# A graph layer and an expert layer on one core: later weight loads, another order in an up product, another order at the end

## The reference

```
h   = item @ W_item.T + b_item                      # 10000 x 128
x1  = x + relu(adj @ h + (layernorm(x) @ W_user.T + b_user))   # adj: 10000 x 10000
n   = layernorm(x1)
cw  = top 2 of softmax(n @ gate_w + gate_b)         # 8 experts, others 0
out = x1 + sum over e of cw[:, e] * (gelu(n @ W1[e] + b1[e]) @ W2[e] + b2[e])
```

## Time and profile before

| what | value |
|---|---|
| median of 3 runs | 1599.41 us (1597.77 to 1600.7) |
| profiled execution | 1598.91 us |
| its span in the trace | 1596.9 us |
| TensorE busy | 1575.2 us, 99% of the span |
| VectorE busy | 1491.0 us, 93% |
| ScalarE busy | 1225.2 us, 77% |
| GpSimd (POOL) busy | 68.5 us, 4% |
| granted clock of TensorE, mean | 0.998 |
| read and written | 488.31 MB, 306 GB/s |

### The profile page before, as it was taken

The page is one execution under the profiler, slowest core; times in us unless marked ns, Lnnn a source line. Parts: engine busy times, 40 slices in busy tenths (PEclk is TensorE's granted clock), DMA queues, the critical chain, the costliest instruction groups (busy, mean ns, idle before and its releaser), DMA issues.

```text
span 1596.9 us, 26046 instructions
## 1 busy us (share of the span) xinstructions
PE 1575.2 (99%) x7085; PEld 1304.3 (82%) x7085; DVE 1491.0 (93%) x2148; ACT 1225.2 (77%) x1419; POOL 68.5 (4%) x63
## 2 busy tenths in 40 slices
PE   8999999999999999999999999999999999999997
PEld 6878888888888888888888888888888888888875
DVE  6989999999999999999999999999999999999987
ACT  5778778787878777878787878777777777777866
POOL 2000000000000000000000000000000000000000
PEclk9999999999999999999999999999999999999999
DMA  9999898989898989898989898989899999989952
GB/s 371 363 324 323 299 328 299 327 299 324 290 332 287 331 290 330 284 336 280 347 281 344 282 340 292 327 296 324 298 319 310 314 315 303 323 298 326 299 201 76
DMA packets 168373, 488.31 MB, mean 306 GB/s; under 512 B 26097, under 2 KB 63858, under 8 KB 168354
## 3 DMA queue, kind: packets, MB, share of 16 engines
q1 hardware_dynamic: 156576, 479.61, 87.4%
q10 hardware_dynamic: 10946, 6.17, 1.2%
q0 software_dynamic: 832, 2.30, 0.4%
HBM read 481.90 MB, written 6.10 MB: 306 GB/s over the span
## 4 chain that ended last, share of the span: by engine, by line
issue 93%; PE 2%; DMA 2%; POOL 1%; DVE 1%; ACT 0%; SPq 0%; POOLq 0%; DVEq 0%; ACTq 0%
POOL moments_sb L431 1%; DMA raw<-in_adj_main 1%; PE acc L901 0%; PE acc L903 0%; PE acc L902 0%; DMA spread_sb<-scales 0%; DVE t_sb L764 0%; DMA r_sb<-t_moments_rows 0%; DVE o_sb L775 0%; ACT a_hi L469 0%; DVE a_lo L640 0%; DVE a_lo L756 0%; DMA t_moments_rows<-turned_sb 0%; SPq L334 0%; PE ps_y L872 0%
## 5 line engine op out<-in xcount | busy, mean ns | idle before, releaser
L469 ACT ACTIVATE a_hi<-raw 128x1000 fp32r<-128x1000 f32 (+1 forms) x800 | 807.4, 1026 | 274.9 <-PE acc L903 193.3
L640 DVE TENSOR_TENSOR a_lo<-raw,a_hi 128x1000 fp32r<-128x1000 f32 x780 | 917.4, 1194 | 46.0 <-ACT a_hi L469 44.9
L901 PE MATMUL acc<-a_hi,h_hi 128*128 128x500 f32 x1560 | 617.7, 396 | 6.3 <-DVE a_lo L640 5.5
L903 PE MATMUL acc<-a_hi,h_lo 128*128 128x500 f32 x1560 | 607.9, 390 | 0.0
L902 PE MATMUL acc<-a_lo,h_hi 128*128 128x500 f32 x1560 | 605.7, 388 | 0.0
L901 PEld LDWEIGHTS acc<-a_hi,h_hi 128*128 128x128 f32 x1560 | 293.8, 188 | 70.7 <-issue 9.6
L902 PEld LDWEIGHTS acc<-a_lo,h_hi 128*128 128x128 f32 x1560 | 294.1, 188 | 62.5 <-issue 4.6
L903 PEld LDWEIGHTS acc<-a_hi,h_lo 128*128 128x128 f32 x1560 | 293.6, 188 | 60.3
L517 ACT ACTIVATE g_sb<-ps_z,b_sb 128x500 f32<-128x500 f32 x304 | 188.0, 669 | 61.9 <-PE ps_y L922 59.7
L756 DVE TENSOR_TENSOR g_lo<-g_sb,g_hi 128x1000 fp32r<-128x1000 f32 x152 | 181.0, 1191 | 5.2 <-ACT g_hi L523 5.1
L523 ACT ACTIVATE g_hi<-g_sb 128x1000 fp32r<-128x1000 f32 x152 | 156.3, 1028 | 0.1
(11 more groups left out here) (134 smaller groups left out, 878.0 us busy)
## 6 DMA issues: line engine op xcount, KB each, us to landing
raw<-in_adj_main SPq DMA_DIRECT2D x780, 500.0 KB, 5.2
spread_sb<-scales SPq DMA_DIRECT2D x160, 250.0 KB, 6.0
xr_sb<-in_xR SPq DMA_DIRECT2D x20, 256.0 KB, 6.6
x_sb<-in_xT SPq DMA_DIRECT2D x20, 250.0 KB, 6.3
xr_sb<-u_moments_rows SPq DMA_DIRECT2D x20, 250.0 KB, 5.3
r_sb<-u_moments_rows SPq DMA_DIRECT2D x20, 250.0 KB, 6.7
xt_sb<-t_moments_rows SPq DMA_DIRECT2D x20, 250.0 KB, 4.9
r_sb<-t_moments_rows SPq DMA_DIRECT2D x20, 250.0 KB, 5.6
```

The costliest lines, as they stand in the source:

```text
L469: nc.scalar.activation(a_hi[q][0:rows, 0:cols], raw[s][0:rows, 0:cols], ACT.Copy).then_inc(hi_ready, 1)
L640: nc.vector.tensor_tensor(low, whole, val(high), ALU.subtract).then_inc(lo_ready, 1)
L901: nc.tensor.matmul(acc[:, 0:T], w_hi, m_hi, start=(k == 0), stop=False)
L903: last = nc.tensor.matmul(acc[:, 0:T], w_lo, m_hi, start=False, stop=False)
```

## The change

It has three parts. POOL waits until three blocks of adj are used before it issues the constants and W1. In an up product the low part of W1 by the high part of xn comes second and the high part of W1 by the low part of xn last; for expert 0 both halves' products with xn's high part come first, then the wait for xn's low part, then the two remaining matmuls. And the written-out orders after pass 19 differ on ScalarE, VectorE and TensorE. SP's and POOL's order is the same.

```diff
+WEIGHTS_FROM = 3
...
         @block.gpsimd
         def _(pool):
             nc.gpsimd.memset(power_sb[:, :], -0.5).then_inc(power_ready, 1)
+
+            pool.wait_ge(adj_used, WEIGHTS_FROM)
             for dst, src in consts:
                 pool.dma_start(dst[:, :], src).then_inc(const_landed, 16)
...
             gelu(rest, 7)
+            high(rest, 7)
             tail(NB, A_NORM)
-            high(rest, 7)
             tail(NB, A_EXP)
             gelu(NB, 0)
             high(NB, 0)
+            tail(NB, A_SEND)
             gelu(NB, 1)
-            tail(NB, A_SEND)
             high(NB, 1)
             gelu(NB, 2)
+            high(NB, 2)
             finish(NB)
-            high(NB, 2)
...
             tail(NB, V_STATS)
+            tail(NB, V_NORM)
             scale(rest, 3)
-            tail(NB, V_NORM)
+            low(rest, 5)
             scale(rest, 4)
             add(rest, 3)
-            low(rest, 5)
+            add(rest, 4)
+            scale(rest, 5)
             low(rest, 6)
-            add(rest, 4)
             tail(NB, V_XN)
-            scale(rest, 5)
+            low(rest, 7)
             tail(NB, V_LOGITS)
-            add(rest, 5)
             tail(NB, V_LO)
-            low(rest, 7)
-            scale(rest, 6)
             tail(NB, V_PROB)
-            add(rest, 6)
             tail(NB, V_COMPARE)
             tail(NB, V_RANK)
             tail(NB, V_WEIGHT)
+            scale(rest, 6)
             low(NB, 0)
+            add(rest, 5)
             scale(rest, 7)
+            add(rest, 6)
             add(rest, 7)
             low(NB, 1)
             low(NB, 2)
             scale(NB, 0)
             scale(NB, 1)
+            low(NB, 3)
             add(NB, 0)
-            low(NB, 3)
+            add(NB, 1)
             scale(NB, 2)
-            add(NB, 1)
             low(NB, 4)
             add(NB, 2)
             scale(NB, 3)
             low(NB, 5)
             add(NB, 3)
             scale(NB, 4)
+            low(NB, 6)
             add(NB, 4)
-            low(NB, 6)
...
                     pe.wait_ge(xn_hi_ready, i)
-                    pe.wait_ge(xn_lo_ready, i)
                 for j in range(HH):
...
                     nc.tensor.matmul(ps_z[j][:, 0:T], w1_hi[:, at:at + P], xn_hi[:, :], start=True, stop=False)
-                    nc.tensor.matmul(ps_z[j][:, 0:T], w1_hi[:, at:at + P], xn_lo[:, :], start=False, stop=False)
-                    nc.tensor.matmul(ps_z[j][:, 0:T], w1_lo[:, at:at + P], xn_hi[:, :], start=False,
-                                     stop=True).then_inc(z_done, 1)
+                    nc.tensor.matmul(ps_z[j][:, 0:T], w1_lo[:, at:at + P], xn_hi[:, :], start=False, stop=False)
+                    if e > 0:
+                        up_low(e, j)
+                if e == 0:
+
+                    pe.wait_ge(xn_lo_ready, i)
+                    for j in range(HH):
+                        up_low(e, j)
+
+            def up_low(e, j):
+                at = e * H + j * P
+                nc.tensor.matmul(ps_z[j][:, 0:T], w1_hi[:, at:at + P], xn_lo[:, :], start=False,
+                                 stop=True).then_inc(z_done, 1)
...
             rest = NB - 1
+            down(rest, 3)
             tail(NB, T_TURN)
-            down(rest, 3)
             down(rest, 4)
```

## The result

The changed kernel takes **1601.62 us**, median of 17 executions (1599.89 to 1603.94). The kernel before took 1598.98 in 17 executions beside them. The ratio is 1.0017, 95% interval 1.001 to 1.0024: 1.6 to 3.8 us slower. The forecast was 1599.4 and "within 3.2 us of no change".

What follows compares the result with a forecast made beforehand. TensorE, busy 99% of the span, was taken as the bound, with a dependency chain deciding the end. Start -1.6 and end +2.1 gave +0.5 on the profiled 1598.91: 1599.4 us, range 1596.2 to 1601.8.

Steps and rivals of the forecast that it cites:

- Weights later: At the start, deferring the constants and W1 shortens TensorE's waits for adj blocks: -1.6 us.
- The bound on block 9: At adj block 9, data arriving at 28.88; half the deferred bytes still to come at 27.4, worth 1.5 us.
- The 0.34 of block 10: TensorE's idle time before adj block 10, 0.34 us, counted as a wait that helps keep the start's lead.
- the 40% I kept to: POOL queue's share of the DMA engines, 0.63 of 1.57 MB, used to price the deferred bytes at block 9.
- Cost 0: In the passes, expert 0's later first half is covered by ScalarE's 0.57 us idle: cost 0; uncovered 3.8 us.
- The end, step by step: Six-step walk of the chain after the last adj block: +2.1 us with half clock, +0.4 with full clock.
- step 6: VectorE's work after the scales land: at half clock scale(1) waits 2.0 us for down(1); end +2.1 us.
- The forecast's case: Clock halves in the 4 us gap before the third up product: +0.5 us, 1599.4, chance 0.45.
- clock holds: Rival: full clock survives the 4 us gap at the end; 1597.7 us, chance 0.25.
- Both ends gain: Rival: block 1 comes earlier and scale(7) is reached earlier, say 1 us; -3.7, 1595.2 us, chance 0.12.
- Deferred bytes only move the wait: Rival: block 9's data still land at 28.88, the lead falls to about 0.3; 1601.4 us, chance 0.13.
- Late half uncovered: Rival: expert 0's later half is not covered in the passes; +3.8 us, 1603.2, chance 0.05.

Runs made afterwards that it cites:

- first experiments: Follow-up runs timed beside the unchanged kernel before; its 35 executions there have a median of 1598.81 us.
- fill run: Changed kernel plus 15 unread matmuls after the last tile's second up product, where TensorE waits for gelu of expert 1: 1599.60 us, ratio 1.001.
- end order: Kernel before with only the three written-out orders after the last pass: 1602.36 us, ratio 1.0019.
- send back: Changed kernel with the send of the scales put back behind gelu of expert 1: 1597.68 us, ratio 0.9993.
- scale first: Changed kernel with the send behind gelu of expert 1, and VectorE's add 5 and scale 7 ahead of expert 0's low part: 1596.41 us, ratio 0.9989.
- weights: Kernel before with only the later loads of the constants and W1: 1597.62 us, ratio 0.9989.
- turn back: Changed kernel with the last tile's four transposes put back ahead of the down product of expert 3: 1599.93 us, ratio 1.0007.
- last only: Scale first with the transposes put back too, and the new up order only in the last tile's expert 0: 1595.63 us, ratio 0.9975.

## Why the prediction was right or wrong

**Weights later: right, with block 9 and block 10 misjudged.** Forecast -1.6; the profile gives -1.28 at the last adj matmul, the run alone -1.2. From block 1 to block 3 the kernel before needs 6.25 us and the eleven profiles with the later loads 4.48 to 4.51, which is the 1.7 of the forecast: blocks 2 and 3 lost their waits and block 1 kept its own. Block 1 itself begins at 12.5 to 14.3 in the eleven and at 13.1 to 13.8 in the three without (a mean of 13.5 in both), so the change doesn't move it; in the profile after it happened to come 0.76 late. Pass 1 began at 86.2 to 87.0 in the eleven, at 87.9 to 88.3 in the three: 1.5 us between the means. The bound on block 9 was wrong: its split came 4.9 us earlier (3.7 to 5.0 in the eleven), and TensorE never waited for it. What was deferred shows at block 12, where TensorE waits 0.14 to 0.66 us in three of the eleven. The 0.34 of block 10 was a misreading: it is idle time of the weight loads (PEld in the earlier trace rows), while the matmuls around it start 0.34 apart in place of 0.22, a loss of 0.12. By the Trainium skill (DMA: Bandwidth & Descriptors, Queues, rings and completion order) each DMA engine takes turns between the queue rows it has work for. POOL's queue had 46% of the bytes from 26 to 32 us (1.08 of 2.34 MB), which is nearer to equal turns than the 40% I kept to. The time did not depend on it.

**Up order in the passes: the step "Cost 0" failed, by little.** The gelu's half was covered, as said, but a pass is 0.02 us longer, 0.4 in all. What in the pass takes it was not looked for and stays open. At the end the order did what was said: four matmuls of expert 0 ran ahead of xn's low part, and that product was done at full clock.

**The end, step by step.** The transposes are 1.07 later (forecast 1.06). down(5) waits 2.03 (1.29 before; from the forecast's times 2.2). The send is where it was (23.16 for 23.22; forecast the same to 0.1 later), for the reason given: scale 7. gelu(1) follows it; the gap is 4.10 (forecast 4). The clock falls in it. The end is 2.18 longer (forecast 2.1). Only the inside of step 6 differs: the matmuls ran at half clock for a little over 3 us and not 5, so scale(1) waited 0.67 and not 2.0; the first scale started 0.67 later than before against the last adj matmul, behind a late low(2), and of three later waits of VectorE for a down product (0.24, 0.30, 0.42) two are new. That is 1.9 of the 2.2. One premise was also misread. I took the half clock of the earlier trace rows to follow 2 us of idle, but in the kernel before it set in earlier, near 1562.4, half a microsecond after the gate's eight matmuls (8 columns each) had ended:

```profile
1561.00:1562.00 1.00, 0.94 (x8) 0.85 (x8) 0.50 (x2) 1.00 (x2) 0.00 (x0) 1.00 0.00 0
1562.00:1563.00 1.00, 0.00 (x0) 0.00 (x0) 0.93 (x4) 0.98 (x2) 0.00 (x0) 0.72 0.00 0
```

**Where the number went wrong: the clock of other executions.** The sum was made for one execution with one fall of the clock, and for that it holds: +0.5 forecast, +1.0 between the two profiled executions. But the changed kernel's profiled execution was the fastest of its 17. By granted clock the others go like this:

```
changed:  0.998  1599.9 (1)   0.997  1601.4 (10)   0.996  1602.3 (3)   0.995  1603.1 (3)
before:   0.999  1597.5 (10)  0.998  1598.8 (12)   0.997  1600.0 (11)  0.995  1602.6 (2)
```

(median us and count; before in the 35 executions of the first experiments). A thousandth of clock is about 1 us in both. The kernel before has 6.4 us at half clock in its profile (0.998) and 7.0 in a mean execution, so its profile is a typical one. The changed kernel has 6.4 in its profile and 11.1 in a mean execution: 4.7 us more. At the median its clock is 0.997, which is 3.2 us more at half clock than in the profile. One fall lasted 3.4 us in the profile after (near 1570.95 to 1574.4), and matmuls at half clock for 3.4 us are 1.7 us late. That is the distance from the profile to the median: by these numbers an execution at the median has one fall more than the profile. The fill run fits this way of counting: it has 5.8 us in place of 11.1, and it lacks the fall of 3.4 and, in its profile, 2.2 of the half clock after the last matmul (0.8 for 3.0).

Where can it be? I had priced the wait of down(5), which grew from 1.3 to 2.0 us, at nothing for the clock. Of the five profiles in which it is 2.0 (changed, end order, send back, fill, scale first) two have a fall right behind it; of the nine in which it is 1.0 to 1.3 none has. And in each of the three pairs of runs that differ only by the transposes, the one with the longer wait has more time at half clock: 11.1 for 9.9, 5.6 for 3.8, 5.2 for 3.8, which points the same way, though not by much. Pass 1's wait, old and left out of the sum, had a fall in five of the fourteen. By these counts, an estimate, an execution has about 0.8 falls (2/5 + 5/14) beside the one in the long gap; the mean's 4.7 us more would be 1.4. So the failed term is **the clock's part of the end**: I gave one fall in one gap, where each longer gap has its own chance of one. In sizes: of the 2.2 us by which the forecast was low, 0.3 are the start, 0.1 the end as profiled, and 1.7 the clock of the other executions. No execution at the median was traced, so that falls fill these 1.7 us is inferred from the clocks, and in which gaps the rest of them lie stays open.

The forecast's case was right by its mechanism, and the effect went to the side of "slower" by 2.6 us, inside the 3.2 that I had called indistinguishable. Seventeen executions of each kernel tell it apart; the bound was too wide. The rivals: "clock holds" is out, since the clock fell in all three profiles with the gap. "Both ends gain" is out, since block 1 kept its wait and the send went no earlier. "Deferred bytes only move the wait" named 1601.4, the nearest number to the measured 1601.62, but by luck: the wait at block 9 was gone, and the loss lies at the end. "Late half uncovered" asked 3.8 us of the passes, which lost 0.4.

## What to carry to other kernels

In an in-order queue a DMA issue that waits for two semaphores (here the gate's weights and the scales of the tile before) stands as long as the later of them, so look at all its semaphores before moving it ahead of compute: here it was moved ahead of a gelu that TensorE needed, while the scale it really waited for came no earlier. Move the work that holds the wait (scale 7, the transposes) first; then the same send goes 2.2 us earlier. Where an end has several gaps of 2 to 4 us without matmuls, price each as a chance of the half clock (gaps of 1.0 to 1.3 us before down(5) had none in nine profiles), and compare many executions, since a single profile shows one draw.

## What the runs showed that I had not expected

- The clock fell behind gaps of 2.0 to 2.1 us in some executions (end order, fill) and not in others with the same gap (changed, send back, scale first). In the gap before gelu of expert 1 it fell in all three profiles that had it at 3.7 to 4.1 us without matmuls (changed, turn back, end order).
- Pass 1's wait for xn, the same code in all kernels, had a fall in it in five of fourteen profiles (weights, end order, turn back, scale first, last only). From the start of pass 1 to the last adj matmul those five took 1461.4 to 1462.7 us and the other nine 1459.4 to 1460.4, so a fall and the longer wait beside it cost 1 to 3 us together, as much as the whole change. TensorE stood 2.1 to 3.5 us there in the five and 1.5 to 2.4 in the nine.
- Deferring 1.23 MB, 3.1 us of transfer, moved block 9's split 4.9 us forward (3.7 to 5.0 over the eleven profiles).
